# Scatters and gathers of a routed expert kernel on one core: paced by TensorE's pairs, or in twos by their own landings

## The reference

```
xn  = layernorm(x)
# branch 1: a recurrence over the sequence, gated
z   = layernorm(xn, ln_w, ln_b)
H_t = tanh(H_{t-1} @ A.T + z_t @ (Ws + Wi).T + bs + bi)        # 16 states
s   = (H @ Wo.T + bo) * sigmoid(z @ Wg.T + bg) + xn
# branch 2: 16 experts, each token takes the 4 best
scores = sigmoid(xn @ gate_w.T);  idx = top_k(scores + gate_b, 4)
w      = 2.5 * scores[idx] / sum(scores[idx])
y      = sum over the 4 of  w_e * (silu(xn @ w1_e.T) * (xn @ w3_e.T)) @ w2_e.T   + shared expert
out    = x + s * silu(y)
```

## Time and profile before

| | us |
|---|---|
| median of 3 runs | 517.19 |
| the three runs | 515.18, 517.19, 518.63 |
| span of the profiled execution | 513.9 |
| TensorE busy | 339.1 |
| VectorE busy | 311.1 |
| GpSimd busy | 265.4 |
| ScalarE busy | 251.0 |

### The profile page before, as it was taken

How to read it: one execution, slowest core, us unless ns; L and a number is a source line. 1 busy time by engine, 2 the same in 40 slices (tenths; PEclk the granted TensorE clock), 3 DMA queues, 4 the chain that set the end, 5 groups by cost and what they waited for, 6 DMA issues and landing times.

```text
span 513.9 us, 10001 instructions
## 1 busy us (share of the span) xinstructions
PE 339.1 (66%) x3107; PEld 261.7 (51%) x3107; DVE 311.1 (61%) x977; ACT 251.0 (49%) x462; POOL 265.4 (52%) x278
## 2 busy tenths in 40 slices
PE   0365566849467786976799968797876968645210
PEld 0352443626355665755698846575654756433100
DVE  4899776676703545545643626786776555346745
ACT  1851666536434455443787746565664644422000
POOL 2005377766646566655600165766555554436773
PEclk9976698797876889888999989999997898676555
DMA  7998499425443566654779768899977777436653
GB/s 247 305 328 281 129 343 331 161 86 201 143 165 127 175 186 201 196 172 156 216 220 269 227 192 268 281 282 285 285 243 211 249 217 225 128 119 194 174 160 126
DMA packets 88675, 109.27 MB, mean 213 GB/s; under 512 B 9649, under 2 KB 78002, under 8 KB 88626
## 3 DMA queue, kind: packets, MB, share of 16 engines
q1 hardware_dynamic: 74656, 74.47, 45.7%
q0 software_dynamic: 12288, 33.57, 20.7%
q10 hardware_dynamic: 1682, 0.59, 0.4%
HBM read 55.91 MB, written 52.69 MB: 211 GB/s over the span
## 4 chain that ended last, share of the span: by engine, by line
PE 35%; another core or an unknown queue 12%; issue 10%; ACT 8%; DVE 6%; POOL 5%; DMA 1%; ACTq 1%; POOLq 0%; DVEq 0%
PE bank L850 13%; PE bank L872 8%; PE bank L656 6%; POOL xn_parts L638 5%; PE bank L863 3%; ACT xn_f L1851 3%; PE bank L898 2%; ACT sh_h L1868 1%; ACT y_ring L1875 1%; ACT xn_f L1859 1%; ACT x_ring L1881 1%; PE bank L948 1%; DVE mix_sb L1371 1%; PE bank L774 1%
## 5 line engine op out<-in xcount | busy, mean ns | idle before, releaser
L638 POOL DMA_INDIRECT xn_parts<-y_slots,slot_u x128 | 127.2, 994 | 126.2 <-PE bank L656 39.6
L619 POOL DMA_INDIRECT x_slots<-xn_parts,slot_u x128 | 131.7, 1029 | 115.1 <-DVE slot_u L1253 36.0
L850 PE MATMUL bank<-w_all,xn_f 128*128 (+1 forms) x864 | 122.2, 295 | 22.2 <-issue 11.5
L850 PEld LDWEIGHTS bank<-w_all,xn_f 128*128 128x128 f16 x864 | 87.3, 106 | 44.8 <-issue 30.6
L1524 DVE SCALAR_TENSOR_TENSOR xn_f<-bank,xn_f 128x256 f32<-128x256 f32 x72 | 30.5, 424 | 111.9 <-ACT xn_f L1859 69.3
L1851 ACT ACTIVATE xn_f<-bank 128x1024 f16<-128x1024 f16 x72 | 73.5, 1022 | 36.7 <-remote 22.3
L872 PE MATMUL bank<-w_all,sh_silu 128*128 (+1 forms) x432 | 68.2, 299 | 5.5 <-ACT y_ring L1875 4.2
L1875 ACT ACTIVATE y_ring<-bank 128x512 f32<-128x512 f32 x72 | 42.9, 596 | 54.4 <-PE bank L872 33.7
L1859 ACT ACTIVATE xn_f<-bank 128x256 f32<-128x256 f32 x72 | 27.5, 382 | 55.0 <-remote 32.4
L656 PE MATMUL bank<-ident_h,w_stage 128*128 128x128 f16 x576 | 48.6, 231 | 1.5 <-issue 1.4
L872 PEld LDWEIGHTS bank<-w_all,sh_silu 128*128 128x128 f16 x432 | 41.8, 106 | 14.5 <-issue 7.5
(11 more groups left out here) (215 smaller groups left out, 456.9 us busy)
## 6 DMA issues: line engine op xcount, KB each, us to landing
w_stage<-x_slots SPq DMA_DIRECT2D x72, 256.0 KB
y_slots<-y_ring SPq DMA_DIRECT2D x72, 256.0 KB
x_slots<-zero_h SPq DMA_DIRECT2D x10, 1024.0 KB
x_ring<-in_x SPq DMA_DIRECT2D x32, 256.0 KB
w_stage<-in_w13t SPq DMA_DIRECT2D x17, 256.0 KB
x_ring<-in_x SPq DMA_DIRECT2D x8, 512.0 KB, 7.7
out<-mix_sb SPq DMA_DIRECT2D x15, 256.0 KB
w_stage<-in_w2t SPq DMA_DIRECT2D x17, 128.0 KB
```

The lines of the kernel that those rows point to most:

```text
L619: eng.indirect_dma_start(out=x_slots, out_offset=bass.IndirectOffsetOnAxis(ap=slot_u[:, n * TOPK + k:n * TOPK + k + 1], axis=0), in_=xn_pa ...
L638: eng.indirect_dma_start(out=fin_y[:, r, j, k, :], out_offset=None, in_=y_slots[0:2 * READY_PAIR[c] * P, :], in_offset=bass.IndirectOffset ...
L850: mm = eng.matmul(gu[:, j * 2 * F:(j + 1) * 2 * F], xg_T[:, n % 2, ((j * 2 + px) * KD + k) * P:((j * 2 + px) * KD + k + 1) * P], weights_o ...
```

## The change

The waits on half pairs go, with their constants. From scatter 61 on, each scatter with an even k (k = 0 and 2) waits until all earlier scatters of its batch have landed, or, where it is the first of its batch, until all 16 of the batch before have. In the first ten units each gather with an even place in its unit waits until the two before it have landed, the first of a unit for the last two of the unit before. Units 10 to 15 have no such waits. The waits of the head, of `slots_made`, of the stored y and of the products stay.

```diff
-    PER_HEAD_STEP, PER_HALF_SCATTER, PER_HALF_GATHER = 1.4, 1.65, 1.3
+    PER_HEAD_STEP = 1.4
     HEAD_FREE = 3
     HEAD_SCATTERS = HEAD_FREE + int(HEAD_FIRST[NB] * PER_HEAD_STEP)
-    SCATTER_HALF, GATHER_HALF = 5, 74
+    UNDER_WAY, PAUSED_UNITS = 2, 10
...
-            def half_pair(h):
-
-                if h % 2:
-                    eng.wait_ge(pair_gu, h // 2 - 1)
-                else:
-                    eng.wait_ge(pair_t, h // 2)
-
-            def beside_scatter(i):
-
+            def beside_scatter(n, k):
+
+                i, b = n * TOPK + k, n // BT
                 if HEAD_FREE <= i < HEAD_SCATTERS:
                     head_step(int((i - HEAD_FREE) / PER_HEAD_STEP))
-                elif i >= HEAD_SCATTERS:
-                    half_pair(SCATTER_HALF + int((i - HEAD_SCATTERS) / PER_HALF_SCATTER))
-
-            def beside_gather(i):
-
-                h = GATHER_HALF + int(i / PER_HALF_GATHER)
-                if h <= 2 * NPAIR:
-                    half_pair(h)
+                elif i >= HEAD_SCATTERS and k % UNDER_WAY == 0:
+                    landed = i - b * BT * TOPK
+                    if landed:
+                        eng.wait_ge(x_slotted[b], 16 * landed)
+                    else:
+                        eng.wait_ge(x_slotted[b - 1], 16 * TOPK * BT)
+
+            def beside_gather(c, i):
+
+                if c < PAUSED_UNITS and i % UNDER_WAY == 0 and c + i:
+                    before, k = (c, i // FT - 1) if i else (c - 1, TOPK - 1)
+                    eng.wait_ge(y_in[before % FIN_RING][k], 16 * FT * (before // FIN_RING + 1))
...
-                        beside_scatter(n * TOPK + k)
+                        beside_scatter(n, k)
...
-                    beside_gather(c * FT * TOPK + i)
+                    beside_gather(c, i)
```

## The result

| | before | after |
|---|---|---|
| median of the runs, us | 517.12 | 611.47 |
| runs, us | 515.18 to 518.63 | 609.88 to 619.57 |
| ratio, 95% interval | | 1.182, 1.177 to 1.186 |

Slower by 18%, in the predicted direction, but 11 us above the range and 43 above the forecast of 568. In all of after's rows lines up to 636 stand two lower than in the kernel before: L617 is the scatter, L636 the gather, L654 the transposition, L848 gate and up, L1573 the combine.

A forecast was written before the change was run, and what follows sets the result against it. Waits between stages, joined by three gates, set the end, no engine being full. Scatters 22.9, clock 2, gathers 40, units 10 and 11 -13.8 make 51.1 on 513.9, 565.0; with 3.3 for the median 568 us, range 545 to 600.

The forecast's parts named there:

- the gates: Three waits join stages: 25th load for last scatter, first gather for last pairs' y, unit 12 for unit 9's product.
- 257.4 + 33 ps + 39 pg: Short form of the predicted span in us, with ps and pg the microseconds for two scatters and for two gathers.
- Gathers, 4.5 us for two: Units 0 to 9: 1.25 issue plus 3.23 landing with wake per two; the 80 gathers take 178 instead of 138 us.
- Scatters, 4.0 us for two: Scatters from 61 on: 1.27 issue, 2.4 landing, 0.3 wake per two; last landing 274.8 against 251.9, +22.9 us.
- The landing against the rule: Check by the skill's rule: 2.3 us per landing, 3.56 us for two, which would mean no change, 513.7 us.
- Tail, costed at nothing: Units 12 to 15, from 464.9 us to the end: 49.0 us that the change doesn't touch.
- 1: Rival, bare landings: two scatters 3.5 us, two gathers 3.97, no loss of clock; 529 us, holds 525 to 545; chance 0.08.
- 2, crowded landings: Rival: pairs' loads and stores delay each two, scatters 4.6, gathers 5.2 us; 615 us, holds 600 to 625; chance 0.07.
- 3: Rival, landing hidden: landing with wake costs no more than old pauses, 3.56 us a two; 512 to 522 us; chance 0.02.
- 4: Rival, relief: spaced indirect DMAs free the pairs; at 3.3 us for both twos 498 us, faster; chance 0.03.
- TensorE's idle time: TensorE stands perhaps 20 us before the 25th load; its clock is then low, so 2 us are added.
- gate one: 25th block load, pair 24, waits at L475 for the last scatter; a later scatter moves the pairs behind one for one.

The follow-up runs named there:

- after_again: The changed kernel, unchanged, measured a second time because the first profiled execution was a disturbed one: 613.7 us, span 611.7.
- scatter_twos: Changed kernel with the old half-pair waits back in front of the gathers, so only scatters go in twos: 558.5 us, 1.073; 503.3 us on the third chip.
- gather_twos: Changed kernel with the old half-pair waits back in front of the scatters, so only gathers of units 0 to 9 go in twos: 583.3 us, 1.119.
- ones: Changed kernel with one under way instead of two, a wait before every scatter from 61 on and every gather of units 0 to 9: 741.6 us, 1.42.
- unpaced: Changed kernel without any pacing wait in front of scatters from 61 on or of gathers: 609.7 us, 1.171.
- gather_unpaced: Scatters as in the kernel before, no pacing wait in front of the gathers: 570.3 us, 1.093.
- unpaced_again: The kernel with no pacing in scatters or gathers, run on the third chip: 442.1 us, 0.994 of the kernel before there.

## Why the prediction was right and wrong

**What bounds the kernel, and the gates: right.** The 25th load goes 0.5 us behind the last landing in *after_again*, the first gather 42.3 behind that load (predicted 42.4, the clock's 2 us in it). Units 10 and 11 take 20.0 (20.7). The structure 257.4 + 33 ps + 39 pg held; the terms in it were mis-sized: 33 x 4.3 + 39 x 5.17 is 343.5 where the prediction had 307.5. Against the predicted span of 564.9, *after_again* is 46.8 longer:

| term | predicted | measured | difference |
|---|---|---|---|
| first added wait ends (scatter 62 starts) | 142.8 | 145.5 | +2.7 |
| 33 twos of scatters, to the last landing | 132.0 | 141.9 | +9.9 |
| to the first gather | 42.4 | 42.9 | +0.5 |
| gathers of units 0 to 9 | 178.0 | 204.1 | +26.1 |
| units 10 and 11 | 20.7 | 20.0 | -0.7 |
| tail | 49.0 | 57.3 | +8.3 |

**Gathers, 4.5 us for two: the step that failed.** The 39 that are waited for take (204.1 - 2.5)/39 = 5.17 on average: 1.32 of issue, 3.12 of landing, 0.73 until GpSimd goes on. That is 26.1 us of the 46.8. The prediction took 3.23 from VectorE's combines in the tail, as landing and wake together. Read from the DMA engines' records, the gathers of the tail land in 3.00 us on average in the kernel before, and in 3.12 in the twos; so the landing was well read, but only 0.23 us were left for a wake. GpSimd goes on 0.62 us behind a landing in most of the twos and 1.1 to 1.2 in a few. The 0.3 of the earlier trace rows is its wake behind a product of VectorE. The upper end, 5.2, was nearly it. The argument that fewer gathers per microsecond bring the traffic down towards the tail's was right: the DMA share fell from 0.81 to 0.60, and the landing from 3.67 on average in the kernel before to 3.12. The third chip shows the same 3.15 at a share of 0.60, and 4.49 in strings at 1.00, where the queue of gathers is in it.

**Scatters, 4.0 us for two: right for an idle TensorE, too low beside pairs.** The first 19 twos take 4.58 us, landing 2.60; the last 13, most of them behind the pairs' stop, 3.97, landing 2.05. The prediction had 2.4 and 0.3, the runs show 2.05 and 0.62 in the quiet: two errors that cancel. Beside the pairs they don't, and a reason was at hand in the prediction itself, which said that the pairs' loads and stores run beside most of them. The first added wait ends 2.7 us late for the same reason: scatter 61 lands 4.4 us behind its issue, and the prediction had 2.6 with the wake. In the sum these two make 12.6 us.

**The landing against the rule.** The scatters' landing in the quiet is 2.05 us and the mean of gathers 3.12. The Trainium skill, "DMA: Bandwidth & Descriptors", section "Anatomy of one DMA — SWDGE (gpsimd) path", gives an estimate of 2.3 for both: right for the one within 0.25, 0.8 too short for the other. It has no wake, which is about 0.7 more on each of 72 twos here.

**Tail, costed at nothing: wrong on two chips.** It is 57.3 us. The last gather is issued 17 us before the end where the kernel before has 8, and there are still moments in it, two of them of 11 us. This row of VectorE in *after_again* is from the tail:

```profile
563.47 0.87 DVE L1573 SCALAR_TENSOR_TENSOR xn_parts<-xn_parts,topk_w,bank 128x256 f32<-128x256 f32 x2 [6.69 <-remote]
```

On the third chip the tail is 48.6. In *scatter_twos* it is 51.1, in *gather_twos* 56.7 and in *ones* 57.2. In the kernels with these long tails units 10 to 15 make one string of 48 gathers, where in the kernel before and in *scatter_twos* GpSimd still waits for products before unit 12. That the string is the cause fits what *unpaced* shows and wasn't tried by itself.

**The rivals.** 1 fell: two scatters take 3.97 us even in the quiet, where it had 3.5, and two gathers 5.17, where it had 3.97. 2, crowded landings (600 to 625, at 0.07), held the time, in part by luck: its price for gathers, 5.2, is the measured one (5.17) for another reason, since of the 0.67 us that a two takes above the forecast, 0.5 are the wake and 0.1 each issue and landing; its 4.6 for scatters fits the twos beside the pairs (4.58, landing 2.60 against 2.05 in the quiet) but not the rest, and the tail brought 8 us more. 3 fell, as two cost 4.33 and 5.17 and not 3.56. 4 was half right: on these chips the pairs do run faster beside twos (231 instead of 253 us for the 23rd), and as predicted can't profit, since scatters would need under 3.3 us for two.

**TensorE's idle time** before gate one was put at 20 us and is 57.5, since the relief brings the pairs there 22 us sooner. It costs nothing by itself: the start of the pairs behind it was already charged, and the 2 us for the clock were enough. The granted clock is 0.50 to 0.57 until 296 us and 1.00 from there, so the few slow pairs were as predicted.

## What to carry to other kernels

A wait that lets a queue of DMAs run empty costs one landing and one wake each time, here 2.7 to 3.3 us for scatters and 3.85 for gathers; count it per drain, with the wake of the engine that waits and not of another. A window that slides bounds the transfers under way at a third of the cost for the scatters (11.5 us against 37.2); with gathers, up to four under way, it did not bound the strings. And a pace that is needed on one chip may do nothing on the next: measure on more than one before an order is changed for strings of DMAs.

## What the runs showed of the hardware that was not expected

- GpSimd goes on 0.62 us behind the landing of its own indirect DMA in most of the twos of *after_again*, and 0.3 us behind a product of VectorE.
- The same program takes 521 to 522 us on two chips (517 in the first measurement) and 442 to 443 on another. Between scatter 62 and unit 12 the changed kernel, which has no strings there, takes the same time on both within 2 us a stage, and the kernel before 61 us more (317.2 and 256.0); in all the changed kernel differs by 15 us (611.7 and 597.0), of them 9.5 before scatter 62 and 8.7 in the tail.
- Beside such strings TensorE, VectorE and ScalarE stop together on those chips, for up to 6.6 us at a time in *unpaced* and 7.2 in *gather_unpaced*, with the DMA engines at a share of 0.29. In that stretch of *unpaced* SyncE issues nothing and no packet but the gathers' moves. On the third chip both go on beside a string: from 282 to 300 us of *unpaced_again* SyncE's queue has 4156 packets beside 607 of the gathers, and issues 16 transfers. What ends the stops isn't in the trace. Why these chips do it and the third does not stays open.
